# Layer 1's routed sum: gathers without addition into used-up weights memory, ranks added by VectorE

## The reference, cut to what matters

```python
x = layernorm(x2)                                   # 2048 x 256
aff = x @ centroids.T                               # 2048 x 64
idx = top_k(aff + expert_biases, 8)
w = sigmoid(take(aff, idx)); w = w / (sum(w) + 1e-8)
y[e] = silu(x @ W_up[e]) @ W_down[e]                # 64 experts, 256 -> 128 -> 256
out = x2 + shared(x) + sum over the 8 chosen e of w[e] * y[e]
```

## Time and profile before

| what | value |
| --- | --- |
| median of 3 runs | 1061.76 us |
| lowest and highest | 1061.12, 1062.68 us |
| the profiled execution's own time | 1056.91 us |
| its span in the trace | 1055.0 us |
| TensorE, VectorE, ScalarE, GpSimd busy | 840.2, 491.9, 383.2, 411.1 us |
| expert loop on TensorE | to about 923 us of the span |

### The profile page before, as it was taken

One profiled execution on the slowest core, in us unless ns is written; L12 is line 12 of the kernel. 1 busy time (PEld: TensorE's weight loads), 2 busy tenths in 40 slices (PEclk: granted clock), 3 DMA queues, 4 the chain that ended last, 5 costly groups with the idle time before them and its releaser, 6 DMA issues.

```text
span 1055.0 us, 21664 instructions
## 1 busy us (share of the span) xinstructions
PE 840.2 (80%) x6226; PEld 725.7 (69%) x6226; DVE 491.9 (47%) x1691; ACT 383.2 (36%) x1374; POOL 411.1 (39%) x401
## 2 busy tenths in 40 slices
PE   5899999899999998899998998599989998900000
PEld 4788887699999976667766666488878987800000
DVE  3666665412211236787787865265444444400002
ACT  1222222311111156565655552156556655500000
POOL 3100000111111111566666556400213078888886
PEclk9899999799999999999999999799999999955555
DMA  8466777799999839722222225577889999965556
GB/s 249 160 238 244 254 269 269 260 299 329 323 328 331 289 94 292 246 88 92 89 90 86 89 81 170 176 222 240 254 265 277 279 268 290 275 103 73 70 85 124
DMA packets 179377, 217.90 MB, mean 207 GB/s; under 512 B 13904, under 2 KB 164688, under 8 KB 179280
## 3 DMA queue, kind: packets, MB, share of 16 engines
q1 hardware_dynamic: 123408, 143.31, 42.0%
q0 software_dynamic: 25344, 44.06, 18.0%
q10 hardware_dynamic: 30528, 29.37, 8.2%
HBM read 126.64 MB, written 90.05 MB: 205 GB/s over the span
## 4 chain that ended last, share of the span: by engine, by line
PE 57%; issue 16%; DVE 10%; DMA 5%; ACT 4%; POOL 4%; POOLq 2%; DVEq 1%; SPq 1%; another core or an unknown queue 0%; ACTq 0%
PE PS L786 11%; PE PS L1034 5%; PE PS L1041 5%; PE PS L796 5%; DMA Q<-queue 4%; PE PS L654 3%; PE PS L672 3%; PE PS L865 3%; PE PS L1022 3%; PE PS L875 3%; ACT R L1238 2%; PE PS L912 2%; POOL Q L1974 2%; PE PS L632 2%; DVE nmax L1576 2%
## 5 line engine op out<-in xcount | busy, mean ns | idle before, releaser
L1974 POOL DMA_INDIRECT Q<-routed,slot x112 | 173.8, 1552 | 63.9 <-issue 32.7
L1923 POOL DMA_INDIRECT queue<-Q,slot x128 | 125.7, 982 | 86.4 <-DVE nmax L1576 53.6
L1034 PEld LDWEIGHTS PS<-Q 128*128 128x128 f32 x768 | 116.8, 195 | 24.4 <-issue 9.3
L1238 ACT ACTIVATE R<-PS,nmax 128x154 f32<-128x154 f32 x256 | 108.3, 547 | 56.5 <-DVE nmax L1576 46.1
L1034 PE MATMUL PS<-Q 128*128 128x128 f32 x768 | 120.5, 280 | 9.9 <-DVE Q L1763 5.2
L786 PEld LDWEIGHTS PS<-R 128*128 128x128 f32 x992 | 115.2, 192 | 4.3 <-issue 2.6
L786 PE MATMUL PS<-R 128*128 128x128 f32 x992 | 116.2, 275 | 1.3 <-ACT R L1200 1.1
L1763 DVE COPY Q<-R 128x256 f32 x192 | 58.2, 304 | 126.1 <-PE PS L1041 86.4
L1041 PE MATMUL PS<-R,Q 128*128 x384 | 116.3, 386 | 0.0
L1307 ACT ACTIVATE Q<-PS 128x128 f32<-128x128 f32 x192 | 53.5, 279 | 99.9 <-PE PS L1041 77.7
L1022 PE MATMUL PS<-ident,Q 128*128 128x128 f32 x384 | 76.9, 283 | 9.8 <-DMA Q<-queue 9.1
(11 more groups left out here) (281 smaller groups left out, 1588.3 us busy)
## 6 DMA issues: line engine op xcount, KB each, us to landing
R<-in_gate_up SPq DMA_DIRECT2D x31, 1024.0 KB
Q<-queue SPq DMA_DIRECT2D x192, 160.0 KB
routed<-pads SPq DMA_DIRECT2D x16, 1536.0 KB, 6.9
routed<-Q ACTq DMA_DIRECT2D x96, 256.0 KB
R<-in_down SPq DMA_DIRECT2D x31, 512.0 KB
queue<-pads SPq DMA_DIRECT2D x16, 640.0 KB, 3.3
R<-in_W_up SPq DMA_DIRECT2D x16, 512.0 KB
R<-in_W_down SPq DMA_DIRECT2D x8, 1024.0 KB
```

Source lines behind the costliest of these rows:

```text
L1034: pe.matmul(up1_bank(j), w_now[:, j % BEHIND, c, :], x1T[:, j % BEHIND, c, :], start=(c == 0), stop=(c == KC - 1))
L1238: i = act.activation(prob[:, g % 2].rearrange("p (k h) -> p h k", h=HG)[:, h, :], src, ACT.Exp, bias=nmax2[:, g % 2, h:h + 1], accum_out=d ...
L1923: pool.indirect_dma_start(out=queue1, out_offset=bass.IndirectOffsetOnAxis(ap=slot1[:, t * TOP1 + k:t * TOP1 + k + 1], axis=0), in_=pay[:, ...
L1974: pool.indirect_dma_start(out=acc[:, t, :], out_offset=None, in_=routed1, in_offset=rows, compute_op=ALU.add).then_inc(S(f"acc_in{t}"), 16)
```

## The change

The list of gathers keeps its order, rank by rank with the smallest place first (now counted r = 0 to 7). Ranks 0 to 6 land without addition, each in a place of its own in `R`: rank r of tile t lies where the weights of expert 8r + t // 2 were, up weights for even t and down weights for odd t. Rank 7 lands in `acc`. The need of a gather is now the larger of two rows: the last that its tokens need, and the end of the expert whose memory it takes. For this VectorE and TensorE get a few more small steps at 4, 8 and 48 of the loop, and empty steps name expert 63 in place of expert 0. After the loop VectorE adds ranks 1 to 6 to rank 0 for eight tiles at a time (12 additions of 128 x 2048), adds that sum to the residual (16 instructions, `most`), and last adds rank 7 (16 instructions, `final`).

```diff
...
     LAG = 14
+    IN_R = TOP1 - 1
+    BIG = float(1 << 15)
     LAND = 4
...
                                "row1", "row_of1", "expert_of1")),
-            ("needs1_psum", ("begin_ps", "lastT_ps", "need_ps")),
-            ("needs1_steps", ("ones1", "begin_col", "begin_diag", "rows1", "last1")),
+            ("needs1_psum", ("begin_ps", "end_row_ps", "lastT_ps", "need_ps")),
+            ("needs1_steps", ("ones1", "begin_col", "begin_diag", "own_zero", "own_expert", "end_col", "end_rows", "rows1", "last1")),
             ("tile_rows_steps", ("moved1", "moved_sel1", "best_rows1")),
-            ("need_steps", ("need_up1", "need_of1")),
+            ("need_steps", ("need_row1", "need_max1", "need_up1", "need_of1")),
...
         x1T, w_now, h1T = q(BEHIND, KC, P), q(BEHIND, KC, F1), q(4, P)
-        tile_rows = q(NT, TOP1)
+        tile_rows = q(TOP1, NT)
         acc = q(NT, D)
-        active1, began1, row_at, ones1, begin_diag = (acc[:, i, 0:n] for i, n in enumerate((NX1, NX1, NX1, P, E1)))
+        active1, began1, row_at, ones1, begin_diag, own_expert, end_col, need_row = (acc[:, i, 0:n] for i, n in enumerate((NX1, NX1, NX1, P, E1, P, 1, P)))
...
             return bank((0, 1, 4)[j % BEHIND])[:, 0:D]
+
+        def sum_part(r, odd):
+
+            at = odd * NUP + r * (NT // 2) * D
+            return R[:, at:at + NT // 2 * D]
+
+        def gathered(r, t):
+            return acc[:, t, :] if r == IN_R else sum_part(r, t % 2)[:, t // 2 * D:(t // 2 + 1) * D]
...
                 pe.matmul(bank(2)[:, 0:E1], ones1[0:E1, :], begin_diag[0:E1, :], start=True, stop=True).then_inc(S("begin_ps"), 1)
+                pe.wait_ge(S("end_rows"), nth("end_rows", 1))
+                pe.matmul(bank(2)[0:1, 3 * P:4 * P], end_col[0:E1, :], own_expert[0:E1, :], start=True, stop=True).then_inc(S("end_row_ps"), 1)
...
                 pe.wait_ge(S("rows1"), nth("rows1", 1))
-                pe.transpose(bank(2)[:, P:2 * P], tile_rows.rearrange("p t k -> p (t k)"), ident[:, :]).then_inc(S("lastT_ps"), 1)
+                pe.transpose(bank(2)[:, P:2 * P], tile_rows.rearrange("p r t -> p (r t)"), ident[:, :]).then_inc(S("lastT_ps"), 1)
...
             dve.tensor_scalar(row_of[:, :], row_at[0:1, :], 0.0, None, ALU.max).then_inc(S("row_of1"), 1)
-            dve.tensor_copy(expert_of[:, :], bank(2)[0:1, 0:NX1]).then_inc(S("expert_of1"), 1)
+            dve.tensor_scalar(expert_of[:, :], bank(2)[0:1, 0:NX1], float(E1 - 1), None, ALU.add).then_inc(S("expert_of1"), 1)
             step("expert_of1")
...
                 dve.memset(ones1, 1.0).then_inc(S("ones1"), 1)
-                dve.tensor_scalar(begin_col[:, :], first, float(P), None, ALU.add).then_inc(S("begin_col"), 1)
+                dve.tensor_scalar(begin_col[:, :], first, float(P) + BIG, None, ALU.add).then_inc(S("begin_col"), 1)
                 step("begin_col")
...
+                dve.memset(own_expert, 0.0).then_inc(S("own_zero"), 1)
+                step("own_zero")
+                mine = IN_R * NT // 2
+                dve.tensor_copy(own_expert[0:E1, 0:2 * mine].rearrange("p (e i) -> p e i", i=2),
+                                ident[0:E1, 0:mine].unsqueeze(2).broadcast_to([E1, mine, 2])).then_inc(S("own_expert"), 1)
+                dve.tensor_tensor(end_col[0:E1, :], start, ntiles, ALU.add).then_inc(S("end_col"), 1)
+                step("end_col")
+                dve.tensor_scalar(end_col[0:E1, :], end_col[0:E1, :], float(P), None, ALU.mult).then_inc(S("end_rows"), 1)
+
             def moved(t):
-                dve.tensor_tensor(row(weight, t), row(weight, t), bank(2)[:, 0:E1], ALU.subtract).then_inc(S("moved1"), 1)
+                dve.tensor_tensor(row(weight, t), bank(2)[:, 0:E1], row(weight, t), ALU.subtract).then_inc(S("moved1"), 1)
                 dve.wait_ge(S("moved1"), nth("moved1", t + 1))
...
                 dve.wait_ge(S("moved_sel1"), nth("moved_sel1", t + 1))
-                dve.max(tile_rows[:, t], row(weight, t)).then_inc(S("best_rows1"), 1)
+                dve.max(tile_rows[:, :, t], row(weight, t)).then_inc(S("best_rows1"), 1)
...
                 dve.wait_ge(S("best_rows1"), nth("best_rows1", NT))
-                dve.tensor_scalar(slot1[:, :], tile_rows.rearrange("p t k -> p (t k)"), -1.0, None, ALU.add).then_inc(S("rows1"), 1)
+                dve.tensor_scalar(slot1[:, :], tile_rows.rearrange("p r t -> p (r t)"), -1.0, BIG - 1.0, ALU.mult, ALU.add).then_inc(S("rows1"), 1)
...
                 step("lastT_ps")
-                dve.tensor_reduce(last_row[:, :], bank(2)[:, P:2 * P], X_AXIS, ALU.max).then_inc(S("last1"), 1)
+                dve.tensor_reduce(last_row[:, :], bank(2)[:, P:2 * P], X_AXIS, ALU.min).then_inc(S("last1"), 1)
...
                 step("need_ps")
-                dve.tensor_scalar(need1[:, :], bank(2)[0:1, 2 * P:3 * P], float(PAIR * P - 1), None, ALU.add).then_inc(S("need_up1"), 1)
+                dve.tensor_scalar(need_row[0:1, :], bank(2)[0:1, 2 * P:3 * P], -1.0, BIG, ALU.mult, ALU.add).then_inc(S("need_row1"), 1)
+                step("need_row1")
+                dve.tensor_tensor(need_row[0:1, :], need_row[0:1, :], bank(2)[0:1, 3 * P:4 * P], ALU.max).then_inc(S("need_max1"), 1)
+                step("need_max1")
+                dve.tensor_scalar(need1[:, :], need_row[0:1, :], float(PAIR * P - 1), None, ALU.add).then_inc(S("need_up1"), 1)
                 step("need_up1")
...
+            def sum_rank(r, odd):
+                for t in range(odd, NT, 2):
+                    dve.wait_ge(S(f"acc_in{t}"), nth(f"acc_in{t}", 16 * (r + 1)))
+                if r > 1:
+                    dve.wait_ge(S("summed"), 2 * (r - 2) + odd + 1)
+                dve.tensor_tensor(sum_part(0, odd), sum_part(0, odd), sum_part(r, odd), ALU.add).then_inc(S("summed"), 1)
+
+            for r in range(1, IN_R):
+                for odd in range(2):
+                    sum_rank(r, odd)
             for t in range(NT):
+                dve.wait_ge(S("summed"), 2 * (IN_R - 2) + t % 2 + 1)
+                dve.scalar_tensor_tensor(X[:, t, :], gathered(0, t), rstd_all[:, t:t + 1], X[:, t, :], ALU.mult, ALU.add).then_inc(S("most"), 1)
+            for t in range(NT):
+                dve.wait_ge(S("most"), t + 1)
                 dve.wait_ge(S(f"acc_in{t}"), nth(f"acc_in{t}", 16 * TOP1))
-                dve.scalar_tensor_tensor(X[:, t, :], acc[:, t, :], rstd_all[:, t:t + 1], X[:, t, :], ALU.mult, ALU.add).then_inc(S("final"), 1)
+                dve.scalar_tensor_tensor(X[:, t, :], gathered(IN_R, t), rstd_all[:, t:t + 1], X[:, t, :], ALU.mult, ALU.add).then_inc(S("final"), 1)
...
             pool.iota(pos1[:, :], pattern=[[P, NX1]], base=-int(FAR), channel_multiplier=0, allow_small_or_imprecise_dtypes=True).then_inc(S("pool_const1"), 1)
-            pool.iota(expert_rep[:, :], pattern=[[0, P]], base=0, channel_multiplier=1, allow_small_or_imprecise_dtypes=True).then_inc(S("pool_const1"), 1)
+            pool.iota(expert_rep[:, :], pattern=[[0, P]], base=1 - E1, channel_multiplier=1, allow_small_or_imprecise_dtypes=True).then_inc(S("pool_const1"), 1)
             pool.iota(region0[:, :], pattern=[[0, 1]], base=0, channel_multiplier=QROWS, allow_small_or_imprecise_dtypes=True).then_inc(S("pool_const1"), 1)
...
             pool.wait_ge(S("need_of1"), nth("need_of1", 1))
-            for k in reversed(range(TOP1)):
+            for r in range(TOP1):
                 for t in range(NT):
-                    i = t * TOP1 + k
+                    i = r * NT + t
                     need = pool.value_load(need1[0:1, i:i + 1], min_val=1, max_val=NX1 // PAIR)
...
                     pool.sem_inc(S("waited_pool"), 1)
-                    rows = bass.IndirectOffsetOnAxis(ap=slot1[:, i:i + 1], axis=0)
-                    if k == TOP1 - 1:
-                        pool.indirect_dma_start(out=acc[:, t, :], out_offset=None, in_=routed1, in_offset=rows).then_inc(S(f"acc_in{t}"), 16)
-                    else:
-                        pool.wait_ge(S(f"acc_in{t}"), nth(f"acc_in{t}", 16 * (TOP1 - 1 - k)))
-                        pool.indirect_dma_start(out=acc[:, t, :], out_offset=None, in_=routed1, in_offset=rows,
-                                                compute_op=ALU.add).then_inc(S(f"acc_in{t}"), 16)
+                    if r:
+                        pool.wait_ge(S(f"acc_in{t}"), nth(f"acc_in{t}", 16 * r))
+                    pool.indirect_dma_start(out=gathered(r, t), out_offset=None, in_=routed1,
+                                            in_offset=bass.IndirectOffsetOnAxis(ap=slot1[:, i:i + 1], axis=0)).then_inc(S(f"acc_in{t}"), 16)
...
```

## The result

The changed kernel takes 1069.4 us (median of 14 runs, 1061.24 to 1074.39) against 1060.88 us for the kernel before (14 runs). The ratio is 1.0086, with a 95% interval of 1.0063 to 1.0109: slower by 0.9%, where 996.4 us had been forecast. The profiled execution has a span of 1069.6 us and 1071.45 us of its own time. The profiled execution of the kernel before was one of its quicker ones (span 1055.0 us), so the two traces lie 14.6 us apart where the medians lie 8.5 apart.

What follows compares the result with a forecast made beforehand. GpSimd's issue of gathers was taken as the bound; 64.8 us (gathers) + 1.1 (end) - 0.5 (loop additions) = 65.4 us less, from 1061.76 to 996.4 us. Its own range was 990 to 1003, widened to 988 to 1010.

Steps and rivals of the forecast that it cites:

- What bounds the kernel: End of the kernel: GpSimd's issue of gathers bounds it, not transfers; 108 gathers at 1.856 us each from 846.45 us.
- The gathers: GpSimd's list: 108 gathers without addition save 0.60 us each, 64.8 us; 1.256 us apart, the last starts at 982.1 us.
- The anchor: Last gather that waits for a stored pair, at 846.45 us; forecast to move later by 0 to 1.2 us, 0.5 taken.
- So no new wait appears.: GpSimd's gathers find their pairs stored in time; the tightest, rank 2 of tile 1, has 15 us to spare.
- The loop is not slowed; if it gets faster, nothing comes of it.: Expert loop's transfers: 61 plain gathers take 0.44 ms of DMA engine time where adding ones took 0.55.
- VectorE's sums.: Behind the loop, from 924.7 us: 12 sums of 2.29 us each run beside the gathers, free with about 2 us slack.
- The tail.: From last gather's start to final product: 2.86 us instead of 3.94; the final product starts at 985.0 us.
- What the loop gets in addition.: Extra small operations at loop steps 4, 8 and 48: between nothing and 1.2 us later, 0.5 us taken.
- The rival that the sums hold up GpSimd: Behind the loop: VectorE's sums stop gather issue, adding 35 us, 1031 in all; loss over 14 us has 6% chance.
- The rival that ends slower: GpSimd's list: a gather tied to a late pair holds all behind it; time 1099 us, chance 2%.

Runs made afterwards that it cites:

- The two kernels with the other sum: Changed kernel, 46 gathers spaced by GpSimd fills, sums in PSUM with one SBUF operand; against the kernel before: 1037.02 us (512 columns), 1033.88 us (320).
- the last kernel: Changed kernel with 320-column fills before 46 gathers and sums moved to PSUM: 1033.88 us, ratio 0.9701 to the kernel before.
- the paced kernel: Changed kernel with an awaited GpSimd fill of 512 columns before each of 46 gathers (places 16 to 61): 1043.04 us, ratio 0.9782 to the kernel before.
- constant waits: Changed kernel without per-gather need loads and signals, one wait for a constant at the head of each rank instead: 1104.15 us, one run.

## Why the prediction was wrong

**What bounds the kernel.** Right for before: the chain of gathers set the end.

**The gathers.** Right: 0.955 us each, 1.256 us apart where nothing holds them. But the last one starts at 1014.57 us, not 982.1. The anchor came 3.6 us later than 846.45, at 850.06, more than the 0 to 1.2 us allowed for; TensorE stands still for 3.2 us from 814.4 us, amid the first plain gathers of rank 1. Behind the anchor the list took 28.9 us longer than at an even 1.256: seven waits for pairs, 13.8 us, are not quite half of it, and longer pauses by "issue" are the rest.

**"So no new wait appears."** The counted needs were right; the times for the pairs assumed a loop at its old pace. Seven such waits appeared, because the pairs themselves were late.

**"The loop is not slowed; if it gets faster, nothing comes of it."** This is the step that failed, and it carried the result. It asked one question, whether the gathers' bytes and packets choke the DMA engines, and answered it rightly: with the loop at its full pace and plain gathers 1.61 us apart their share was 0.97, against 1.10 before. It took the engine time of the transfers for all that a gather can cost others. The issue of gathers has a price of its own: below some distance between 1.45 and 1.61 us, the loop's engines get their semaphores late, as the trace reads. With the gathers at 1.256 us the loop ended 101.8 us later. The row that could have warned showed only 1.856 us, with the loop running well; the forecast took the loop's pace at 1.256 us from it as given, and the range held nothing for it. I had named no rival in which the loop, as the cover, ends late: all of them started with VectorE free at 924.7 us.

**VectorE's sums.** Their size was right: 2.283 us against 2.29. That they are free was not, once the loop ended at 1025.3 us: the cover was gone, and all 39.3 us came to the path.

**The tail.** Forecast 2.86 us from the last gather to the final product. The changed kernel can't show it, since VectorE came later. The two kernels with the other sum do: 1029.99 to 1033.61 us with a fill of 512 columns, 3.62 us, and 1016.83 to 1020.85 us with 320, 4.02 us. The lone gather at 376.88 us was no measure for it; the adding gather's 3.94 us was nearer. In a kernel that had run as forecast this would have cost 0.8 to 1.2 us, an estimate from these two.

**What the loop gets in addition.** It can't be read within 1 us; the last kernel's loop ends at 921.8 us with all of it.

**The rival that the sums hold up GpSimd** did not decide here, as the gathers were through before the sums began, but the paced kernel shows that its mechanism is real. The longest gathers took 2.35 and 1.90 us under two sums and 4.05 us under the products that follow. The prediction judged it by a product of 0.48 us, which left a gather at 1.55 us. But that product had started 0.30 us after the gather, as all 14 that overlap a gather in that trace start 0.10 to 0.32 us after it; the case that costs, a gather that starts second, did not occur there. The Trainium skill ("SBUF — State Buffer", section "Who interferes with whom") names a VectorE instruction with two SBUF inputs as what blocks a GpSimd instruction that reads SBUF. The 2.35 us, and the 1.075 us once one input lies in PSUM, agree with that. Its inferred exemption of descriptor generation does not hold for these gathers.

**The rival that ends slower**, a wait of GpSimd at a need that comes out late, is not what happened. The sign of slower came by another way.

What stays open: what in the issue of a gather delays the semaphores of other engines. The runs leave out the place where it lands, its rows and bytes, the full DMA engines, the needs' register loads and signals, and the changed loop steps. They show that the distance from start to start decides, since seven kernels at 1.61 us and above keep the loop going and five at 1.45 us and below don't, most of them seen in one run each. That something else grows with it, such as the length of an unbroken row of close gathers, is not excluded: with constant waits the loop fared worse at the same distance. The link itself, events some 0.7 us apart in a standstill, is read from the traces and was not changed by itself. Gathers issued in another way, or fewer of them with more rows each, were not tried. Nor is it settled what makes the "issue" pauses of 1.1 to 3.3 us behind the loop; slow register and semaphore instructions on GpSimd's own sequencer go with them.

## What to carry to other kernels

A slow instruction on an engine off the loop's path may be what keeps the loop running; before making it faster, ask what its higher rate does to those who share queues and semaphores with it, and give the forecast a case for it. When a whole set of engines waits at once and no queue is full, look at who goes on undisturbed: here GpSimd, one gather after another. Then a deliberate delay, only where there is something to protect, is worth a try: 46 fills brought back the 100 us of loop and left 2.2% of gain, 3.0% with the other sum.

## What the hardware showed unexpectedly

- While plain indirect DMAs start 1.22 to 1.45 us apart, the engines of the expert loop stand still again and again, for up to 21.6 us at a time; at 1.61 us the longest gap is 3.4 us.
- TensorE's granted clock follows: 0.68 and 0.63 in the changed kernel's held-up stretches, 1.00 from 850 to 925 us with the gathers 1.61 us apart. The gaps are thus paid for twice.
- A VectorE addition of 128 x 2048 takes 2.28 us with both operands in SBUF and 2.29 with one in PSUM, but only the first stretches gathers that start under it, from 0.95 to 2.35 us: each of 12 ended 0.82 or 0.83 us after the sum did.
- Half the rows in a gather shorten it from 0.955 to 0.912 us only.
